# Slot attention between two routed FFNs: float32 key sums, value sums by a scan, the softmax centre as a bias, the state copied whole and masked by GpSimd

## The reference

```
q, k  = rope(x @ Wq), rope(x @ Wk);  v = x @ Wv;  g = x @ Wg
sk,sv = clip(x @ sk_w1 @ sk_w2 + sk_b2), clip(x @ sv_w1 @ sv_w2 + sv_b2)   # 4 heads x 64 slots each
wk    = exp(sk);  zk = cumsum(wk over time)
S     = mask(q k^T)
logits= (S @ wk) * scale / zk
p     = softmax(logits over slots)
wv    = exp(sv);  zv = cumsum(wv over time)
A     = mask((p / zv) @ wv^T)
o     = A @ v, normed per head, times silu(g), @ Wo
```

## Time and profile before

| | us |
|---|---|
| median of 3 runs | 506.77 |
| the profiled execution | 506.91 |
| its span, first to last instruction | 504.9 |
| attention, first to last full loop step | 218.5 to 319.5 |

### The profile page before, as it was taken

One profiled execution on the slowest core, in us unless ns is written; L12 is line 12 of the kernel. 1 busy time (PEld: TensorE's weight loads), 2 busy tenths in 40 slices (PEclk: granted clock), 3 DMA queues, 4 the chain that ended last, 5 costly groups with the idle time before them and its releaser, 6 DMA issues.

```text
span 504.9 us, 12339 instructions
## 1 busy us (share of the span) xinstructions
PE 446.7 (88%) x3879; PEld 313.0 (62%) x3895; DVE 433.5 (86%) x1139; ACT 316.5 (63%) x683; POOL 166.0 (33%) x199
## 2 busy tenths in 40 slices
PE   0787899999999775999999999975899999999996
PEld 0444566666666463788888888764456666666664
DVE  3699999999999963799999999975899999999996
ACT  3544455555555476889898989845555555555553
POOL 2999990000000236466666666633000000000000
PEclk9999999999999987799999999995999999999999
DMA  6222000000000000000000000000000000000002
GB/s 214 87 70 81 1 1 0 0 0 0 0 0 1 1 2 0 2 0 1 1 1 0 0 0 0 0 1 1 1 1 2 0 0 0 0 0 0 0 0 83
DMA packets 6697, 6.98 MB, mean 14 GB/s; under 512 B 818, under 2 KB 5170, under 8 KB 6676
## 3 DMA queue, kind: packets, MB, share of 16 engines
q1 hardware_dynamic: 6532, 6.33, 4.2%
q10 hardware_dynamic: 144, 0.39, 0.2%
HBM read 5.67 MB, written 1.05 MB: 13 GB/s over the span
## 4 chain that ended last, share of the span: by engine, by line
PE 55%; DVE 20%; ACT 10%; issue 8%; POOL 4%; DMA 1%; DVEq 1%; POOLq 0%; ACTq 0%
PE bank L1131 16%; PE bank L1143 10%; PE bank L1145 10%; PE bank L1144 10%; DVE h L807 4%; DVE h_lo L813 2%; ACT gate_s L313 2%; ACT qk_t L382 2%; DVE x L796 2%; DVE stats L705 1%; DVE pz L937 1%; PE bank L1325 1%; POOL rstd L543 1%; ACT slot_b L362 1%; ACT h_hi L318 1%
## 5 line engine op out<-in xcount | busy, mean ns | idle before, releaser
L318 ACT ACTIVATE h_hi<-h 128x512 f16<-128x512 f32 x144 | 90.7, 630 | 133.0 <-DVE h L807 133.0
L807 DVE SCALAR_TENSOR_TENSOR h<-bank,gate_s 128x512 f32<-128x512 f32 x144 | 99.4, 690 | 25.5 <-ACT gate_s L313 19.7
L1131 PE MATMUL bank<-w_hi,h_hi 128*128 (+1 forms) x576 | 104.9, 219 | 15.1 <-DVE h_lo L813 10.4
L1143 PE MATMUL bank<-xt_hi,w_hi 128*128 128x512 f16 x288 | 110.6, 384 | 0.0
L1144 PE MATMUL bank<-xt_hi,w_lo 128*128 128x512 f16 x288 | 110.4, 383 | 0.0
L1145 PE MATMUL bank<-xt_lo,w_hi 128*128 128x512 f16 x288 | 110.2, 383 | 0.0
L1131 PE MATMUL bank<-w_hi,h_lo 128*128 (+1 forms) x576 | 104.4, 219 | 0.0
L1131 PE MATMUL bank<-w_lo,h_hi 128*128 (+1 forms) x576 | 104.4, 219 | 0.0
L813 DVE TENSOR_TENSOR h_lo<-h,h_hi 128x512 f16<-128x512 f32 x144 | 102.4, 711 | 0.1
L796 DVE SCALAR_TENSOR_TENSOR x<-bank,wts,x 128x128 f32<-128x128 f32 x288 | 86.5, 343 | 1.3 <-PE bank L1131 0.9
L313 ACT ACTIVATE gate_s<-bank 128x512 f32<-128x512 f32 x144 | 83.4, 579 | 0.0
(11 more groups left out here) (160 smaller groups left out, 851.7 us busy)
## 6 DMA issues: line engine op xcount, KB each, us to landing
wf<-in_w_ffn SPq DMA_DIRECT2D x8, 384.0 KB, 3.1
x<-in_x SPq DMA_DIRECT2D x4, 256.0 KB, 4.8
out_dram<-x SPq DMA_DIRECT2D x4, 256.0 KB, 2.3
cst<-in_consts SPq DMA_DIRECT2D x1, 455.0 KB, 5.1
wf<-in_w_ffn ACTq DMA_DIRECT2D x1, 384.0 KB, 4.0
wqkvg<-in_w_qkvg SPq DMA_DIRECT2D x1, 256.0 KB
wslots<-in_w_slots SPq DMA_DIRECT2D x3, 64.0 KB
wo<-in_w_out SPq DMA_DIRECT2D x1, 64.0 KB
```

The lines of the kernel that those rows point to most:

```text
L318: act.activation(h_hi[:, g, ih, :], h32[:, ih, :], ACT.Copy).then_inc(hhi_done, 1)
L807: nc.vector.scalar_tensor_tensor(h32[:, ih, :], up_ps[ih][:, :], HS / (XS * WS), gate_s[:, ih, :], ALU.mult, ALU.mult).then_inc(hmul_done, 1)
L1131: i = mm(dst, hp[:, g, ih, c * P:(c + 1) * P], wcols(wp, e, at, D), start=(k == 0), stop=(k == 3 * IH - 1))
L1143: mm(ps[:, :], wcols(w_hi, e, at, P), xt_hi[:, ts], start=True, stop=False)
```

## The change

Six edits, all in the attention stage. In PSUM the banks stay where they were.

- **Key sums in float32.** The bf16 parts and their four functions go. `running_sums` and `add_sums` are one float32 product of 256 columns each, with the triangle tables as they are in `cst`.
- **Value sums by a scan.** A new VectorE function `value_sums` scans the turned value slots in PSUM along time, 128 columns for each pair of heads, starting from the last sum of the chunk before. `sums_log` and `sums_product` become two instructions of 256 columns each.
- **Softmax.** `soft_centre` goes; `soft_exp` becomes four activations of 64 columns whose bias is the head's minimum of the negated logits. `soft_scale` takes in the scale.
- **Turning p.** `turn_p` turns the probabilities before they are divided; `prob_scale` divides after it, out of PSUM, and writes `p_t`; `copy_p` goes.
- **State.** `copy_state` is one activation of 384 columns into `state_raw`; GpSimd's new `mask_state` multiplies it with a table of zeros and ones into `state`.
- **Orders.** All four lists of `attn_step` change.

```diff
@@ ScalarE
             def sums_log(c, p, n):
...
-                act.activation(slot_ln[:, :], sum_ps[:, :], ACT.Ln).then_inc(S["sums_ln"], 1)
+                act.activation(slot_ln[:, 0:HM], ksum_ps, ACT.Ln)
+                act.wait_ge(S["v_summed"], c + 1)
+                act.activation(slot_ln[:, HM:2 * HM], v_sums[:, p, :, :].rearrange("p a t -> p (a t)"), ACT.Ln).then_inc(S["sums_ln"], 1)
...
             def copy_state(c, p, n):
                 if n >= 1:
                     act.wait_ge(S["back_done"], c)
                     if n >= 2:
-                        act.wait_ge(S["o_done"], c - 1)
...
+                        act.wait_ge(S["state_copied"], c - 1)
+                    act.activation(state_raw[:, :], state_ps[:, 0:HM + 4 * DK], ACT.Copy).then_inc(S["raw_copied"], 1)
...
             def soft_exp(c, p, n):
-                act.wait_ge(S["centred"], c + 1)
+                act.wait_ge(S["min_done"], c + 1)
...
-                act.activation(prob[:, :], logit_c[:, :], ACT.Exp, scale=-DK ** -0.5).then_inc(S["prob_done"], 1)
+                for h in range(H):
+                    hs = slice(h * M, (h + 1) * M)
+                    i = act.activation(prob[:, hs], logit[:, hs], ACT.Exp, scale=-1.0, bias=logit_min[:, h:h + 1])
+                i.then_inc(S["prob_done"], 1)
@@ ScalarE attn_step
                     copy_o(*end)
-                if front:
-                    slots_high(*front)
+                if mid:
+                    copy_value_slots(*mid)
                 if front:
                     slots_exponent(*front)
-                if mid:
-                    copy_value_slots(*mid)
                 if front:
                     copy_qk_parts(*front)
                 if mid:
                     soft_exp(*mid)
-                if front:
-                    slots_middle(*front)
                 if last:
                     o_square(*last)
                 if front:
                     copy_q(*front)
-                if mid:
-                    copy_p(*mid)
@@ GpSimd
+            def mask_state(c, p, n):
+                if n >= 1:
+                    pool.wait_ge(S["raw_copied"], c)
+                    if n >= 2:
+                        pool.wait_ge(S["o_done"], c - 1)
+                    nc.gpsimd.tensor_tensor(state[:, p, :], state_raw[:, :], blocks[:, :], ALU.mult).then_inc(S["state_copied"], 1)
@@ GpSimd attn_step
+                if mid:
+                    mask_state(*mid)
                 if front:
                     rope_add(*front)
                 if front:
                     qk_low(*front)
-                if front:
-                    slots_rest(*front)
                 if last:
                     gate_o(*last)
-                if front:
-                    slots_low(*front)
                 if last:
                     root_o(*last)
@@ VectorE
+            def value_sums(c, p, n):
+                dve.wait_ge(S["vslot_turned"], c + 1)
...
+                for a in range(2):
+                    i = nc.vector.tensor_tensor_scan(v_sums[:, p, a, :], ones32[:, :], vslot_t_ps[:, a * P:(a + 1) * P],
+                                                     v_sums[:, 1 - p, a, P - 1:P], ALU.mult, ALU.add)
+                i.then_inc(S["v_summed"], 1)
...
             def prob_scale(c, p, n):
-                dve.wait_ge(S["prob_done"], c + 1)
...
+                dve.wait_ge(S["p_turned"], c + 1)
+                dve.wait_ge(S["sums_inv"], c + 1)
...
+                nc.vector.scalar_tensor_tensor(p_t[:, p, :, :].rearrange("p a t -> p (a t)"), p_t_ps, -1.0, slot_inv[:, p, HM:2 * HM],
+                                               ALU.mult, ALU.mult).then_inc(S["p_scaled"], 1)
```

More of the change, by code:

```diff
@@ L1003, in attn_step @@
                 front, mid, last, end = stages(i, n)
+                if mid:
+                    value_sums(*mid)
                 if front:
                     rope_multiply(*front)
+                if end:
+                    norm_apply(*end)
                 if front:
                     clip_slots(*front)
-                if end:
-                    norm_apply(*end)
+                if mid:
+                    sums_product(*mid)
+                if mid:
+                    sums_inverse(*mid)
                 if last:
@@ L1021, in attn_step @@
                     soft_min(*mid)
-                if mid:
-                    soft_centre(*mid)
+                if end:
+                    add_y(*end)
                 if last:
@@ L1026, in attn_step @@
                 if mid:
+                    prob_total(*mid)
+                if mid:
                     prob_scale(*mid)
-                if mid:
-                    prob_total(*mid)
                 if last:
                     norm_squares(*last)
-                if end:
-                    add_y(*end)
+                if front:
+                    mask_s(*front)
                 if last:
@@ L1256, in running_sums @@
             def running_sums(c, p, n):
-                pe.wait_ge(S["slots_b3"], c + 1)
+                pe.wait_ge(S["slots_exp"], c + 1)
                 if n == 0:
                     pe.wait_ge(S["low_lo_done"], NG)
-                for k, part in enumerate((slot_b1, slot_b2, slot_b3)):
-                    i = mm(sum_ps[:, :], tri16[:, :], part[:, p, :], start=(n == 0 and k == 0), stop=True, skip_group_check=True)
-                i.then_inc(S["sums_done"], 1)
+                mm(ksum_ps, tri, slots[:, p, 0:HM], start=(n == 0), stop=True, skip_group_check=True).then_inc(S["sums_done"], 1)
             def logits_of_earlier(c, p, n):
@@ L1283, in add_sums @@
                 pe.wait_ge(S["sums_prod"], c + 1)
-                for part in (slot_b1, slot_b2, slot_b3):
-                    mm(sum_ps[:, :], rest16[:, :], part[:, p, :], start=False, stop=True, skip_group_check=True)
+                mm(ksum_ps, rest, slots[:, p, 0:HM], start=False, stop=True, skip_group_check=True).then_inc(S["sums_added"], 1)
             def add_state(c, p, n):
                 if n >= 1:
-                    pe.wait_ge(S["state_copied"], c)
+                    pe.wait_ge(S["raw_copied"], c)
                 mm(state_ps[:, 0:HM], qk[:, p, D:2 * D], slots[:, p, 0:HM], start=False, stop=True, skip_group_check=True)
@@ L1363, in attn_step @@
                     outputs(*last)
+                if front:
+                    scores(*front)
                 if mid:
-                    add_sums(*mid)
+                    turn_p(*mid)
                 if mid:
                     add_state(*mid)
-                if mid:
-                    turn_p(*mid)
-                if front:
-                    scores(*front)
             pe.wait_ge(consts_loaded, 16)
```

126 lines of the change are left out of this document (51 added, 75 removed).

## The result

| | us |
|---|---|
| kernel before, median of 4 runs beside the change | 506.88 |
| changed kernel, median of 4 runs (524.49 to 525.64) | 525.28 |
| ratio | 1.0335 (95% interval 1.0307 to 1.0362) |
| its profiled execution | 525.03 |
| its span | 522.9 |

The change made the kernel slower by 18.4 us, where +9.8 was forecast and 523 was the upper end of the range. The direction and the place were right and the size was not.

A forecast was written before the change was run, and what follows sets the result against it. Cycles of waits between engines were taken as the bound, 8.42 us a step before and 9.15 after: +9.0 over 13 steps, -0.9 first steps, +2.1 end, -0.4 bias, +9.8, so 516.7 us; range 506 to 523.

The forecast's parts named there:

- The rival "TensorE's freed 0.4 us shows": Attention loop: GpSimd keeps out of the way, step 8.00 us, kernel faster at 500.4 us; chance 0.13.
- the rival "level": Attention loop: both low bounds hold, other waits eat the rest, 8.4 to 8.5 us a step; chance 0.04.
- the ring: Changed attention loop: cycle of waits from exponentials through VectorE, GpSimd and TensorE back to them, 9.15 us a step.
- "slower still": Attention loop: exponentials 0.33 us apart, +0.36 a step, kernel 522 us; slow scans would add 2.2; chance 0.09.
- L290's pace: ScalarE softmax: basis for the four exponentials, an instruction with pointers; 0.333 us each, 0.24 apart, 1.05 for four.
- the L420 pace: ScalarE softmax: alternative basis, 64-column copies that hardly overlap; the four exponentials would take 1.26 us.
- The stall of L985: VectorE's norm_variance, shut out by GpSimd's slots_low: 0.82 us in the old loop, forecast to fall to 0.15.
- the ring of the kernel before: Old attention loop: cycle of waits from norm_apply through TensorE, GpSimd and VectorE back to it, 8.41 us a step.
- qk_low 0.67 and 0.13 in which `sums_inverse` shuts it out: GpSimd's qk_low in the new loop: 0.67 us of its own plus 0.13 shut out by VectorE.
- less 0.4 for the bias of the method: Total for the kernel: queue write-out gave 8.46 for the old step measured at 8.42, so +10.2 became +9.8.
- The forecast of -0.9 for the first two steps: Start of attention: first two steps have no root to wait for and lighter sums, 0.9 us saved.
- The rival "TensorE drops to the lower of its clock levels": Attention stage: new TensorE idle gaps lower its clock, +50 us, about 560; chance 0.02.

The follow-up runs named there:

- the four tests: Changed kernel with norm_variance before mask_s (521.21 us); rope_add before mask_state (544.27); one exponential with VectorE centre (514.67); each scan issued twice (531.35).
- a_scan_twice: Changed kernel with each value scan issued a second time into an unused tile; 531.35 us, ratio 1.0427.
- b_low_first: Kernel before with slots_low ahead of gate_o on GpSimd; 507.32 us, ratio 0.9985.
- b_turn_later: Kernel before with turn_o behind logits_of_earlier on TensorE; 507.32 us, ratio 0.9981.
- a_warm: Changed kernel with products of zeros on TensorE in the first four attention steps; 522.61 us, ratio 1.0274.
- the second execution: Changed kernel profiled and timed once more, unaltered; 524.26 us, ratio 1.0319.
- a_best: Changed kernel with one exponential and VectorE centre, prob_invert and norm_variance ahead of mask_s, sums_inverse behind mask_a; 508.78 us, ratio 1.0016.
- a_mask_late: Changed kernel with rope_add ahead of mask_state on GpSimd; 544.27 us, ratio 1.0712.
- a_six_copies: Changed kernel with the state copied by six small ScalarE copies and mask_state removed; 521.22 us, ratio 1.0241.

## Why the prediction was right and wrong

**Right: what sets the step.** The rival "TensorE's freed 0.4 us shows" and the rival "level" are out. The chain root_o, mask_state, rope_add, qk_high, qk_low, turn_qk, copy_qk_parts, exponentials, turn_p, prob_scale, mask_s, norm_variance is in the timeline, and the four tests moved the step as the ring said: 9.10 (9.05 expected), 10.24 to 10.50 (10.5), 8.75 (8.75), 9.65 to 9.79 (up to 9.7). These expectations start from the measured 9.40, so they test which instructions lie on the ring and not its length. The measured time lies above the 522 of the rival "slower still" too, but not by its mechanism: the exponentials are 0.24 apart, not 0.33, and the scans cost nothing (a_scan_twice).

**Right: single terms.** The exponentials at L290's pace (1.05 us; the L420 pace would have given 1.26): the Trainium skill ("ScalarE: Activation LUTs", section on what ACT_TABLE_LOAD costs) gives 0.333 for one by its formula, and this trace agrees with 0.335. The root, turn and copy terms came within 0.06, the end of the stage at +2.4 against +2.1, and no cost of the setup shows. The stall of L985 is gone as said.

**Wrong off the ring, and without effect.** The scans were taken at 0.33 each and take 0.455. VectorE was to stay under 7.5 us of work and is busy for 7.71 a step. TensorE was to have 0.4 us less work, about 7.4 in all; its busy time, which is another measure than the sum of its products, is 8.00 a step, as before. The 0.88 for four copies of L420 is not in the earlier trace rows, which give 10.2 us in 12 steps, or 0.85.

**Less sure than it was told: the ring of the kernel before.** It was read as closing in "8.41 us, the measured step", but the exchanges of b_low_first and b_turn_later got back 0.07 and 0.04 of the 0.2 and 0.3 that this reading gave. The forecast for the changed kernel does not rest on it, since the new ring was added up by itself, and the old step was measured.

The spans differ by 18.0, and 9.8 was forecast. The missing 8.2 us come in four parts.

**Wrong: the sizes of ring terms, 3.3 us.** By the links of the sum, from the timeline of after:

| link | forecast | measured |
|---|---|---|
| exponentials to prob_scale | 0.51 | 0.53 |
| prob_scale to root_o | 1.32 | 1.37 |
| root_o, mask_state, rope_add, to qk_high | 2.87 | 2.91 |
| qk_high, qk_low, to turn_qk | 1.64 | 1.81 |
| turn_qk to copy_qk_parts | 0.78 | 0.81 |
| copy_qk_parts, exponentials | 2.03 | 1.97 |
| sum | 9.15 | 9.40 |

The step that failed here is "qk_low 0.67 and 0.13 in which `sums_inverse` shuts it out": it is shut out for 0.28 (0.95 in all), so this one overlap makes 0.15 of the 0.25. The range had no bound for such an overlap, although show L985 losing 0.67 us to one. The next largest error is `mask_state`, 1.00 for 0.92. The other links were 0.02 to 0.05 short and the last one 0.06 long. Over 13 steps 0.25 makes 3.3.

**Wrong: the correction, 1.2 us.** The step of before was written out as 8.46 and measured as 8.40 in the middle of the loop. Taking 8.46 off the 9.15 instead of 8.40 made the 13 steps 0.8 too short, and "less 0.4 for the bias of the method" took the same surplus off a second time, since it was already in the 8.46. The surplus was not a property of the method either: for the changed kernel it erred the other way. Counted over all 13 steps of the kernel before (109.67, or 8.44 each) the surplus is only 0.3; the rest is then the third and fourth distances of the changed kernel, which take 19.41 and not twice 9.40, with the clock at 0.50 from 220 to 224.

**Wrong: the first steps, 1.8 us.** The forecast of -0.9 for the first two steps came from rows of the loop, at full clock. Both kernels start the attention at the lower level: 0.53 from 199.5 to 209.3 in both. But the kernel before is back at full clock from 209 on and the changed one from 214, and it falls again from 220 to 224. The first two distances of scores took 9.78 and 7.80 in the kernel before and 8.59 and 9.85 in the changed one, so the changed kernel lost 0.86 where it was to win 0.9. a_warm shows 1.2 us of that in the first distance; the second stays open. The rival "TensorE drops to the lower of its clock levels" was priced for the whole stage, at 50 us and 0.02, where it belonged into the sum as a term of a few microseconds in the first steps.

**Left over: 1.9 us.** 1.45 lie before the first scores. Part of that is chance: the changed kernel's profiled execution reached the second norm 3.5 us late, in a stage that is unaltered, and had made up two of them by the first scores; the second execution was not late there and came to its first scores at 200.28, 0.77 behind the kernel before. Over all fourteen profiles the first scores start at 198.95 to 201.92, in no order of the kernels, so none of the 1.45 can be put down to the change. The end of the stage was 0.3 longer than forecast, the rest 0.17.

## What to carry to other kernels

Where several engines are each over 90% busy, look for the ring before the sum of work: follow one instruction back to itself through waits and queue orders, and ask of each edit what it does to that ring and which new one it closes. Here the edits took 20 us of work from ScalarE and 19 from GpSimd, and cost 18, because three things together closed a longer ring: a 1 us instruction went ahead of the rope on the engine that had the most idle time (0.4 us a step come back without it), four short exponentials took the place of one on the path (0.65), and `norm_variance` went behind `mask_s` (0.3). In a_best the 1 us instruction is still there and the kernel is level, so what such an instruction costs depends on what else stands on its ring. Write the queues out with durations of the rows. Starting from the measured 9.40, that foretold the ordinary step of seven experiments to within 0.15 us; from the kernel before alone it missed by 0.25, and for the two exchanges in the kernel before by 0.13 and 0.26. Give each meeting of GpSimd with a VectorE instruction that shuts it out its full length as an upper bound.

## What the runs showed of the hardware

- A scan of 128 columns on VectorE takes 0.455 us and two in a row 0.82 to 0.85, against 0.28 for a tensor_tensor of that width (L851). The Trainium skill ("DVE: opcode table, instruction layouts, handler registers and perf-mode slots", its paragraph on feedback) says that this scan runs at half throughput; the trace agrees in kind, with 0.17 us more for 128 columns.
- The mutual shut-out of VectorE and GpSimd lengthens whichever comes second, by what is left of the first less 0.12 to 0.14 us: `qk_low` 0.67 to 0.95 with 0.42 of `sums_inverse` left, `norm_apply` 0.28 to 0.77 with 0.62 of `mask_state` left, and L985 0.15 to 0.82 with 0.79 of L625 left. `gate_o` went from 0.46 to 0.69 in b_turn_later.
- TensorE's clock fell after the first steps too, in three of the fourteen profiles. In a_mask_late one distance of 12.54 stands among ones of 10.25 to 10.50; the granted clock is 0.65 from 280 to 290 and 0.84 from 290 to 300, and 1.00 in the ten before and after. TensorE had waited for 1.94 us before 270.7 and for 2.17 before 281.2. a_scan_twice has one step of 10.72 (clock 0.72 from 308 to 314) and a_six_copies one of 10.34, its last (0.76 from 325 to 332), and there no wait of TensorE in the 8 us before was over 0.6 us. What set them off is open.
- The first FFN, the same in all fourteen profiles, let the second norm begin at 168.2 to 169.0 us in eleven of them and at 171.7 to 172.2 in three. Times that differ by less than 1% need several executions here.
